# Another loop order in ScalarE's evictions of q, k and v in a layer of attention and experts

## The reference

```python
xn = _layernorm(x)                       # x: 8 x 4096 x 1024
x = x + attn(xn) + ffn(xn)

# attn: 16 heads of 64
q = xn @ Wq + bq                         # 1024 -> 1024
kv = (xn @ Wdown + bdown) @ Wup + bup    # 1024 -> 256 -> 2048
k, v = split(kv.reshape(B, T, 16, 128), 2)
q, k = rope(q), rope(k)
att = softmax(einsum('bthd,btgd->bthg', q, k) / 8)   # between the heads of one token
out = einsum('bthg,btgd->bthd', att, v) @ Wout + bout

# ffn: top-1 of 8 experts, each 1024 x 1024
probs = softmax(xn @ router_w.T + router_b)
out = (expert_w[argmax(probs)] @ xn + expert_b) * max(probs)
```

## Time and profile before

| | us |
|---|---|
| median of 2 runs | 4222.06 (4220.84 to 4223.27) |
| the profiled execution | 4210.95 |
| its span, slowest core | 4209.4 |
| span over the 8 cores | 4186.1 to 4209.4 |

### The profile page before, as it was taken

One profiled execution on the slowest core, in us unless ns is written; L12 is line 12 of the kernel. 1 busy time (PEld: TensorE's weight loads), 2 busy tenths in 40 slices (PEclk: granted clock), 3 DMA queues, 4 the chain that ended last, 5 costly groups with the idle time before them and its releaser, 6 DMA issues.

```text
span 4209.4 us, 38363 instructions; the slowest of 8 cores (4186.1 to 4209.4 us)
## 1 busy us (share of the span) xinstructions
PE 1951.1 (46%) x16558; PEld 1581.6 (38%) x16558; DVE 796.0 (19%) x945; ACT 1274.6 (30%) x898; POOL 35.0 (1%) x74
## 2 busy tenths in 40 slices
PE   0112363553717363553717363553717363553727
PEld 0111253342616252442616252442616252442615
DVE  2111112212211112212211112212212112212211
ACT  0212514224060514224060514224060514224060
POOL 0000000000000000000000000000000000000000
PEclk9655576675858586775858586775858585775858
DMA  4444031130405031130404031130404031230403
GB/s 145 145 170 160 30 125 56 63 118 1 180 0 180 0 138 43 65 115 0 180 0 180 0 135 45 68 113 1 180 0 180 0 141 40 73 108 1 170 0 130
DMA packets 42363, 366.41 MB, mean 87 GB/s; under 512 B 5059, under 2 KB 6083, under 8 KB 24532
## 3 DMA queue, kind: packets, MB, share of 16 engines
q1 hardware_dynamic: 32980, 330.40, 21.5%
q0 software_dynamic: 9216, 33.56, 2.5%
HBM read 330.39 MB, written 33.55 MB: 86 GB/s over the span
## 4 chain that ended last, share of the span: by engine, by line
PE 37%; ACT 21%; DMA 16%; DVE 10%; ACTq 9%; issue 4%; DVEq 3%; SPq 1%; POOL 0%; POOLq 0%
DMA exbuf<-exscratch 10%; ACTq L471 8%; PE psb L753 7%; PE psa L753 7%; ACT vdm L545 7%; ACT koct L540 7%; PE psb L692 5%; DMA y_f<-exw 4%; PE psb L671 4%; ACT qoct L522 3%; PE psa L649 3%; PE psb L736 2%; DVEq L198 2%; DVE pav L430 2%; PE psa L736 1%
## 5 line engine op out<-in xcount | busy, mean ns | idle before, releaser
L692 PE MATMUL psb<-lat,wup_sb 128*128 128x256 bf16 x1024 | 224.8, 411 | 705.5 <-ACTq L471 705.5
L753 PE MATMUL psb<-xe,exbuf 128*128 128x256 bf16 x4096 | 482.4, 277 | 89.3 <-DMA exbuf<-exscratch 88.5
L753 PE MATMUL psa<-xe,exbuf 128*128 128x256 bf16 x4096 | 468.1, 273 | 0.0
L753 PEld LDWEIGHTS psb<-xe,exbuf 128*128 128x128 bf16 x4096 | 400.9, 99 | 163.0 <-issue 109.2
L692 PEld LDWEIGHTS psb<-lat,wup_sb 128*128 128x128 bf16 x1024 | 141.8, 143 | 786.1 <-issue 728.9
L753 PEld LDWEIGHTS psa<-xe,exbuf 128*128 128x128 bf16 x4096 | 400.8, 98 | 46.4
L492 ACT ACTIVATE lnv<-mv,epsc 128x2 f32<-128x2 f32 x16 | 4.8, 300 | 1317.9 <-DVEq L198 1317.9
L522 ACT ACTIVATE qoct<-psb 64x2048 bf16<-64x2048 f32 x32 | 278.7, 8708 | 225.9 <-PE psb L671 225.7
L540 ACT CAST koct<-psb 128x2048 bf16<-128x2048 f32 x32 | 278.2, 8692 | 124.5 <-PE psb L692 124.5
L545 ACT CAST vdm<-psb 64x2048 bf16<-64x2048 f32 x32 | 278.3, 8696 | 120.8 <-PE psb L692 120.8
L439 DVE TENSOR_TENSOR xe<-xnf,mrep 128x2048 bf16<-128x2048 bf16 x96 | 117.6, 1225 | 900.1 <-PE psa L753 900.1
(11 more groups left out here) (119 smaller groups left out, 1876.6 us busy)
## 6 DMA issues: line engine op xcount, KB each, us to landing
exbuf<-exscratch SPq DMA_DIRECT2D x128, 2048.0 KB, 8.3
y_f<-exw SPq DMA_DIRECT2D x64, 512.0 KB
x_t<-x POOLq DMA_DIRECT2D x32, 512.0 KB, 6.1
exscratch<-exbuf SPq DMA_DIRECT2D x8, 2048.0 KB, 9.0
out<-outsb POOLq DMA_DIRECT2D x32, 512.0 KB, 6.9
y_f<-wq SPq DMA_DIRECT2D x8, 512.0 KB
y_f<-wo SPq DMA_DIRECT2D x8, 512.0 KB
y_f<-wup SPq DMA_DIRECT2D x2, 1024.0 KB
```

The lines of the kernel that those rows point to most:

```text
L692: li = tensor.matmul(out=psb[:, 256 * gch:256 * (gch + 1)], lhsT=wup[:, 4096 * k + 128 * ch: 4096 * k + 128 * (ch + 1)], rhs=lat[:, 256 * ...
L753: li = tensor.matmul(out=pout(m), lhsT=exbuf[:, eb + 1024 * k + 128 * m: eb + 1024 * k + 128 * (m + 1)], rhs=xe[:, xb + 256 * k:xb + 256 * ...
```

## The change

In the three evictions the loops over source and destination are taken in another order. Elements, buffers, number of instructions and waits are the same. Before, an instruction goes through a block's 256 tokens and then to the next block. After, it goes through the 8 blocks of a token and then to the next token. The whole diff:

```diff
                 for hl in range(2):
-                    srcq = re(psb[64 * hl:64 * hl + 64, :], "p (cc og j) -> p cc og j",
+                    srcq = re(psb[64 * hl:64 * hl + 64, :], "p (cc og j) -> p og j cc",
                               og=32, j=8)
                     dstq = re(qoct[64 * hl:64 * hl + 64, :],
-                              "p (og j cc two) -> p two cc og j", j=8, cc=8,
-                              two=2)[:, hl]
+                              "p (og j cc two) -> p og j cc two", j=8, cc=8,
+                              two=2)[:, :, :, :, hl]
                     scalar.activation(out=dstq, in_=srcq, func=AF.Identity, scale=0.125)
...
                     if r < 2:
-                        srck = re(psb[:], "p (g og j) -> p g og j", og=32, j=8)
-                        dstk = re(koct[:], "p (og j gg) -> p gg og j", j=8,
-                                  gg=16)[:, 8 * r:8 * r + 8]
+                        srck = re(psb[:], "p (g og j) -> p og j g", og=32, j=8)
+                        dstk = re(koct[:], "p (og j gg) -> p og j gg", j=8,
+                                  gg=16)[:, :, :, 8 * r:8 * r + 8]
                         scalar.copy(out=dstk, in_=srck)
                     else:
-                        srcv = re(psb[0:64, :], "p (g og j) -> p g og j", og=32, j=8)
-                        dstv = re(vdm[:], "p (og j gg) -> p gg og j", j=8,
-                                  gg=16)[:, 8 * (r - 2):8 * (r - 2) + 8]
+                        srcv = re(psb[0:64, :], "p (g og j) -> p og j g", og=32, j=8)
+                        dstv = re(vdm[:], "p (og j gg) -> p og j gg", j=8,
+                                  gg=16)[:, :, :, 8 * (r - 2):8 * (r - 2) + 8]
                         scalar.copy(out=dstv, in_=srcv)
```

## The result

| | us |
|---|---|
| before, median of 8 runs | 4220.07 (4205.80 to 4226.53) |
| changed, median of 9 runs | 3560.47 (3553.24 to 3608.82) |
| ratio | 0.844, 95% interval 0.8424 to 0.8456 |
| profiled execution of the changed kernel | 3563.36 (before: 4210.95) |

The kernel is 15.6% faster. The forecast was 3526 us with a range from 3430 to 3750.

A forecast was written before the change was run, and what follows sets the result against it. The kernel was taken as a relay with one engine working at a time. From 4210.95 us, evictions (655.7) and clock (40) came off, giving 3515; the median's 11 us offset made 3526, range 3430 to 3750.

The forecast's parts named there:

- The bare relay: q, k and v evictions: nothing hides them, so each us an eviction loses is a us of the tile.
- Write side, k and v: Evictions of k and v: writing eight adjacent elements (16 bytes) takes 1.87 us an instruction instead of about 8.70.
- q: q's evictions: elements 4 bytes apart, eight in 32 bytes, also taken at 1.87 us an instruction.
- Rival C: q's evictions stay at 8.70 us because their bf16 are never adjacent; 219 us back, 3745 us; 8%.
- Read side: Evictions' PSUM reads 1024 bytes apart cost nothing extra, as with L580's 64-byte step.
- B: Evictions' reads across PSUM banks cost one more cycle an element, 164 us, giving 3690 us; 10%.
- D: Evictions: 1024-byte reads cost what the old writes did, or writes never cost; no change, 4222 us; 7%.
- E: Evictions' reads across banks cost more than 4.24 ns an element; slower, 4386 us one step beyond; 7%.
- Covers: Work under the evictions and rounds (PE's down projection, DVE's q and k additions, expert weight and x loads) stays covered.
- The clock: L692's four PE rounds: shorter gaps could catch the 2.4 GHz clock; 40 us less, of at most 108.

The follow-up runs named there:

- test copies: Kernel before, with copies of 2048 elements in various read and write patterns added in the first tile alone; 4394.23 us (one execution).
- e8_after_again: The changed kernel itself run once more, unaltered, for a common chip; 3564.57 us without its slow run, ratio 0.8449.
- e7_adj_fill: Changed kernel with q's even heads adjacent, then odd; spare matmuls after L692's first three rounds (8 each) and before the first (20); 3469.02 us, ratio 0.822.
- e2_kv_only: Changed kernel with q's eviction put back to the old loop order, only k and v new; 3756.14 us, ratio 0.8872.

## Why the prediction was right, point by point

**The bare relay** was right. What was taken off an eviction left the time: k and v alone gave 476 us where their durations and L692's matmuls said 473; q alone gave 214 where its durations said 201, 13 us more than they explain.

**Write side, k and v**: right, 1865 and 1858 ns against 1.87 us. **q**: the term was mis-sized. The step that failed is "I take 1.87, since runs of eight are kinder than L580's pairs". L580 writes whole 4-byte words; q's elements are single halves of words, which cost 4.4 ns per 16 bytes visited. Rival C had named the right feature (never adjacent) but not the size: q kept neither 8.7 nor 1.87 us but 2.43, since four of its elements share 16 bytes: 512 visits at 4.41 ns and the 166 ns on top give 2.42 us. The term came to 197.1 us instead of 179.5, 17.6 us short.

**The Trainium skill's rule for SBUF** (SBUF — State Buffer, Door 1: The DMA port swizzle) asks for two accesses in 16 bytes for full speed. For whole words these runs nearly agree: fp32 cost 1970 ns with two in each 16 bytes and 3742 with one. For single bf16 they do not: at a step of 8 bytes they have two in each 16 and cost 4682 ns against 1866. By that rule q would be at 1.87 us; the measurement decides.

**Read side**: right. The forecast carried L580's 64 bytes over to 1024 without a row at that step; the test copies now show 1866 ns from 8 to 2048 bytes. B, D and E fell with it. The Trainium skill's rule against the change (Advanced Engine Details and Errata, PSUM Cachelines) speaks of matmuls. For reads by ScalarE and VectorE these runs show no such cost (1866 ns, and 2292 against 2286), and whether TensorE's writes pay it no run here shows.

**Covers**: right. The rounds came at gaps of 2.1 to 2.2 us as forecast, except the first: 4.56 us instead of near 3.5; q's dearer pair of evictions, 2 x 0.569 = 1.14 us, accounts for it. DVE's additions for q and k began at 2036.42 in that tile and ended before 2041, under the two rounds of v, and the latent's matmuls lay under q's eviction.

**The clock**: right in direction, mis-sized. 24.0 us came instead of 40; the third taken of the bound of 108 was a guess. The forecast doubted the full 108 because PE would be busy for only about half of the time; the fill confirms that the idle time withholds the rest, for with all gaps filled L692 takes 224.8 - 122.0 = 103 us less than before.

**Not in the sum**: 13.2 us more in L671, L736, L767 and the experts' transfers. With 17.6 and 16 this makes 46.8 of the 48 us between the sum for the profiled execution (3515) and its time (3563.36). Why these 13.2 us came is not shown, and in part they are scatter: in e8_after_again, the same kernel, L767 takes 47.7 us, less than the 49.8 before, and the wait for the transfers 96.5. Against the median (3560.47) the forecast misses by 34 us and not by 48, because the profiled execution of the kernel before lay 11 us under its median and that of the changed kernel 3 us over: that part is luck.

## What to carry to other kernels

Where an instruction permutes on the way from PSUM to SBUF, put the gaps on the PSUM side and let the SBUF side be written in whole 4-byte words without gaps: reading PSUM was free at every step tried (8 to 2048 bytes), writing single bf16 cost up to 5 times as much. A duration per element far above that of a plain copy of the same size is the sign to look for. When an engine's stall is cut in a relay, look at TensorE's clock in what follows: filling the three gaps of 2.1 us with spare matmuls was worth 1.1% here (ratio 0.8449 to 0.8354), and filling all four gaps, the first of 3.4 us included, 1.9% (0.8375 to 0.822, with q's words whole).

## What the runs showed of the hardware

- Writes to SBUF by ScalarE: 1.73 ns for each 16 bytes visited in whole words, 4.4 ns where a word is written in half (4.41 and 4.42 in two differences). VectorE takes the same times where both were tried (2423, 4681, 8692 ns in halves; 3808 against 3816 in whole words at 32 bytes). A step of 32 bytes is somewhat cheaper (8694 ns) than 16 or 128 (9205, 9261), for which no run gives a reason.
- Pairs of bf16 at a step of 16 bytes: 1952 ns when they fill a word, 4682 when they straddle two.
- Reads of SBUF by ScalarE cost 1.75 ns per 16 bytes visited (3790 ns at a step of 16 bytes, 2002 at 8); reads of PSUM cost nothing extra (1866 at 8, 64, 1024 and 2048 bytes).
- TensorE's four rounds ran at 1.2 GHz or partly so with gaps of 2.1 to 2.2 us in the tile of the changed kernel (granted clock 0.50 to 0.94), and at 2.4 GHz with gaps of 1.3 us in that of e7_adj_fill (1.00). A gap of 2.2 us does not decide by itself: in e2_kv_only one round behind such a gap took 1.91 us.
